# Attention with a written-out head loop: values of two tiles in one group, three score banks, and five tiles of each head summed by adding DMAs instead of TensorE

## What is computed

```python
scores = jnp.einsum('bhqd,bhkd->bhqk', q, k) * scale
probs = jax.nn.softmax(scores, axis=-1)
ctx = jnp.einsum('bhqk,bhkd->bhqd', probs, v)
```

## Time and profile before

| | |
|---|---|
| time, median of 3 runs | 2860.41 us (2859.59 to 2862.24) |
| profiled execution, its own time | 2861.7 us |
| span of its trace | 2859.9 us |
| PE busy (matmuls) | 2749.7 us, 96% |
| POOL busy | 1732.3 us, 61% |
| DVE busy | 1628.8 us, 57% |
| ACT busy | 1291.3 us, 45% |
| mean granted TensorE clock | 0.976 of full speed |

### The profile page before, as it was taken

One profiled execution on the slowest core, in us unless ns is written; L12 is line 12 of the kernel. 1 busy time (PEld: TensorE's weight loads), 2 busy tenths in 40 slices (PEclk: granted clock), 3 DMA queues, 4 the chain that ended last, 5 costly groups with the idle time before them and its releaser, 6 DMA issues. The chain is left out here.

```text
span 2859.9 us, 43470 instructions
## 1 busy us (share of the span) xinstructions
PE 2749.7 (96%) x13776; PEld 1609.4 (56%) x13776; DVE 1628.8 (57%) x2553; ACT 1291.3 (45%) x2299; POOL 1732.3 (61%) x406
## 2 busy tenths in 40 slices
PE   7999999999799999999999999999999999997999
PEld 6888887778344444444444444444444444436887
DVE  8411110111778777867777768767867777724231
ACT  3111111110066666656656656656656666672100
POOL 0111111110199989988989989889988998982111
PEclk9999999999599999999999999999999999998999
DMA  3233223112611121112111211221112111004332
GB/s 140 107 121 110 110 110 111 66 66 89 162 27 41 35 60 36 41 36 59 39 39 43 52 35 42 50 46 35 42 36 60 38 39 34 9 16 143 125 106 92
DMA packets 145917, 189.29 MB, mean 66 GB/s; under 512 B 87152, under 2 KB 112240, under 8 KB 134896
## 3 DMA queue, kind: packets, MB, share of 16 engines
q1 hardware_dynamic: 145712, 186.70, 23.5%
HBM read 122.44 MB, written 63.69 MB: 65 GB/s over the span
## 5 line engine op out<-in xcount | busy, mean ns | idle before, releaser
L859 DVE TENSOR_REDUCE part_max<-ps_b 128x1 f32<-128x512 f32 x2048 | 1275.9, 681 | 423.3 <-PE ps_b L740 420.3
L706 POOL TENSOR_TENSOR psum_p<-psum_p,probs 128x2048 f32<-128x2048 f32 x316 | 1457.7, 4613 | 30.4 <-ACT probs L837 0.5
L837 ACT ACTIVATE probs<-ps_b 128x512 f32<-128x512 f32 x2048 | 1115.6, 597 | 754.4 <-PE ps_b L730 724.3
L730 PE MATMUL ps_b<-qp,kp 97*128 97x512 f32 x2048 | 877.1, 432 | 1.5 <-ACT probs L837 1.5
L740 PE MATMUL ps_b<-kp,qp 96*128 96x512 f32 x2048 | 767.0, 417 | 62.6 <-DVE part_max L859 24.0
L730 PEld LDWEIGHTS ps_b<-qp,kp 97*128 97x128 f32 x2048 | 385.6, 189 | 622.1 <-ACT probs L837 460.3
L758 PE MATMUL ps_b<-probs,vh 128*32 128x512 f32 x4096 | 552.3, 611 | 2.6
L740 PEld LDWEIGHTS ps_b<-kp,qp 96*128 96x128 f32 x2048 | 399.1, 195 | 162.4 <-DVE part_max L859 68.1
L232 POOL TENSOR_TENSOR wlo<-wraw,whi 128x1024 fp32r<-128x1024 f32 x29 | 69.4, 2394 | 611.5 <-ACT whi L335 611.5
L261 PE MATMUL ps_a<-xhi,whi 128*128 128x512 f32 (+1 forms) x928 | 370.2, 399 | 1.0 <-DVE elo L424 0.9
L261 PE MATMUL ps_a<-xhi,wlo 128*128 128x512 f32 (+1 forms) x928 | 367.1, 396 | 0.0
(11 more groups left out here) (72 smaller groups left out, 1093.0 us busy)
## 6 DMA issues: line engine op xcount, KB each, us to landing
kp<-qk_scr SPq DMA_DIRECT2D x96, 256.0 KB, 4.1
qp<-qk_scr SPq DMA_DIRECT2D x96, 256.0 KB, 6.2
qk_scr<-ehi SPq DMA_DIRECT2D x16, 1024.0 KB, 3.9
qk_scr<-elo SPq DMA_DIRECT2D x16, 1024.0 KB, 6.7
wraw<-wcat SPq DMA_DIRECT2D x29, 512.5 KB, 7.5
craw<-cz_scr SPq DMA_DIRECT2D x16, 768.0 KB, 5.1
stage<-x SPq DMA_DIRECT2D x16, 512.0 KB, 4.5
v_scr<-elo SPq DMA_DIRECT2D x16, 512.0 KB, 3.3
```

Source lines behind the costliest of these rows:

```text
L706: pool.tensor_tensor(acc[:, :], (acc if n else probs[0])[:, :], probs[t % RING][:, :], ALU.add) \
L730: pe.matmul(ps[:, st_bank(g, j, b), :], kp[j][0:PACK + 1, t * P:(t + 1) * P], qp[j][0:PACK + 1, b * NQ:(b + 1) * NQ], start=True, stop=Tru ...
L837: act.activation(probs[t % RING][:, b * NQ:(b + 1) * NQ], ps[:, st_bank(g, j, b), :], ACT.Exp, scale=SCALE).then_inc(exp_done, 1)
L859: dve.tensor_reduce(part_max[jn % 2][:, tn, b:b + 1], ps[:, MAX_BANK + bank, :], AX_X, ALU.max) \
```

## The change

- All loops of `attend` are written out; there is no `Fori` left in it.
- Values of two tiles (t-2 and t-1) are computed in one group after every even step; transposed scores rotate over three banks (`n % 3`). The last head keeps one tile a step.
- Scores, the transposed maxima and the sums of a head share one ring of four banks in the order of use (`ring_order`); whoever comes to a bank waits for the reader of the unit four places before it (`wait_ring`).
- No tile is summed by TensorE except in the last head. POOL adds ten tiles into `psum_p` (nine additions). The exp of tile 0 is written to a tile of its own, `psum_q`, and five DMAs issued by POOL add tiles 2, 5, 8, 11, 14 onto it (`accum_op=ADD`, 128x2048 float32, 1 MB each), each waiting for the one before. TensorE multiplies `psum_q` and `psum_p` by ones after step 4 of the next head.
- `LEAD` (how many steps the maxima run ahead) is 4, was 3; three slots of q, k, v, were four. ACT takes the sums after step 5, the reciprocal comes after the maxima of step 9, and the product is cut into four instructions of 128x128, after the second maximum of steps 10, 11, 12 and 13.

```diff
-POOL_TILES = [0, 1, 2, 3, 4, 6, 7, 8, 9, 11, 12, 14]
+BASE_TILE = 0
+CHAIN_TILES = [2, 5, 8, 11, 14]
+POOL_TILES = [1, 3, 4, 6, 7, 9, 10, 12, 13, 15]
-LEAD = 3
-POOL_SUMS_AT, TAKE_SUMS_AT, RECIPROCAL_AT, NORMALISE_AT = 3, 4, 8, 10
+LEAD = 4
+SUMS_AT, TAKE_SUMS_AT, RECIPROCAL_AT, NORMALISE_AT = 4, 5, 9, 10
-        ST_BANKS, MAX_BANKS = 2, 4
-        MAX_BANK, PV_BANK, SUM_BANK = 2, 6, 7
+        ST_BANKS, RING_BANKS = 3, 4
+        RING_BANK, PV_BANK = 3, 7
+        def wait_ring(eng, u):
+            n = ring_place[u] - RING_BANKS
+            if n < 0:
+                return
+            kind, h = ring_order[n][:2]
+            if kind == "max":
+                eng.wait_ge(mx_free, maxima_until[n + 1])
+            elif kind == "sum":
+                eng.wait_ge(sums_taken, h + 1)
+            else:
+                eng.wait_ge(neg_ready, h + 1)
...
+            def chain(h, t):
+                if t == CHAIN_TILES[0]:
+                    pool.wait_ge(pv_done, TT * h + BASE_TILE + 1)
+                wait(pool, chained, chain_count(h, t) - 16)
+                pool.wait_ge(exp_done, 64 * h + 4 * t + 4)
+                pool.sem_inc(cleared, 1)
+                pool.dma_start(psum_q[h % 2][:, :], tile(h, t)[:, :], accum_op=ALU.add).then_inc(chained, 16)
+            for h in range(HEADS):
+                for t in range(TT):
+                    if h < LAST and t in CHAIN_TILES:
+                        chain(h, t)
+                    if t in pool_tiles(h)[1:]:
+                        add(h, t)
...
+            def sums(h):
+                u = ("sum", h, 0, 0)
+                wait_ring(pe, u)
+                pe.wait_ge(chained, chain_count(h, CHAIN_TILES[-1]))
+                sum_of(ring_bank(u), psum_q[h % 2], True, False)
+                pe.wait_ge(pool_done, pool_count(h, POOL_TILES[-1]))
+                sum_of(ring_bank(u), psum_p[h % 2], False, True).then_inc(sum_ready, 1)
+            def step(h, t):
+                for b in range(QB):
+                    if h >= 0:
+                        scores_t(h, t, b)
+                    if has_maxima(h, t):
+                        scores(h, t, b)
+                if h < 0:
+                    return
+                if t == 0 and h >= 1:
+                    values(h - 1, TT - 2)
+                    values(h - 1, TT - 1)
+                if h < LAST:
+                    if t % 2 == 0 and t >= 2:
+                        values(h, t - 2)
+                        values(h, t - 1)
...
+                if t == SUMS_AT and h >= 1:
+                    sums(h - 1)
...
+            for h in range(-1, HEADS):
+                for t in range(first_step(h), TT):
                     for b in range(QB):
+                        if has_maxima(h, t):
+                            take_max(h, t, b)
+                        if b == 1 and h >= 1 and 0 <= t - NORMALISE_AT < QB:
+                            normalise(h - 1, t - NORMALISE_AT)
+                    if t == RECIPROCAL_AT and h >= 1:
+                        reciprocal(h - 1)
```

More of the change, by code:

```diff
@@ L527, in attend @@
         psum_p = [sb(f"psum_p{s}", [P, T]) for s in range(2)]
+        psum_q = [sb(f"psum_q{s}", [P, T]) for s in range(2)]
         raw_ctx = [sb(f"raw_ctx{s}", [P, NQ]) for s in range(2)]
@@ L585, in target @@
[L585 to L618, removed]
+        def target(h, t):
+            return (h + 1, t + LEAD) if t + LEAD < TT else (h + 2, t + LEAD - TT)
@@ new lines, in has_maxima, with first_step @@
+        def has_maxima(h, t):
+            return target(h, t)[0] < HEADS
+        def first_step(h):
+            return 0 if h >= 0 else -LEAD
+        ring_order = []
+        for h in range(-1, HEADS):
+            for t in range(first_step(h), TT):
+                if has_maxima(h, t):
+                    ring_order += [("max", h, t, b) for b in range(QB)]
+                if t == SUMS_AT and h >= 1:
+                    ring_order.append(("sum", h - 1, 0, 0))
+                if t == TRANSPOSED_AT and h < LAST:
+                    ring_order.append(("flip", h + 1, 0, 0))
@@ L620, in attend, with tile @@
+        def tile(h, t):
+            return psum_q[h % 2] if based(h, t) else probs[slot(h, t)]
+        previous = {}
+        held = {}
+        for h in range(HEADS):
+            for t in range(TT):
+                if not based(h, t):
+                    previous[h, t] = held.get(slot(h, t))
+                    held[slot(h, t)] = (h, t)
         block = ctx.enter_context(nc.Block())
@@ L761, in values @@
+                if not (h == LAST and t in LAST_ONES_TILES):
                     last.then_inc(pv_done, 1)
-            def sums(g, j, t):
-                mine = tiles(g, j)[1]
-                if t not in mine:
-                    return
-                if t == mine[0]:
-                    wait(pe, sums_taken, number(g, j))
-                for b in range(QB):
-                    last = pe.matmul(ps[b * HD:(b + 1) * HD, SUM_BANK, :], ones[:, :],
-                                     probs[t % RING][:, b * NQ:(b + 1) * NQ], start=(t == mine[0]), stop=False)
-                last.then_inc(pv_done, 1)
@@ new lines, in _ @@
+            for h in range(-1, HEADS):
+                if h >= 0:
+                    pe.wait_ge(negmax_loaded[h % SLOTS], 16 * (h // SLOTS + 1))
+                for t in range(first_step(h), TT):
+                    step(h, t)
+                    if t == TRANSPOSED_AT and h < LAST:
+                        transpose_max(h + 1)
+            values(LAST, TT - 1)
+            last_sums(TT - 1)
+            pe.wait_ge(pool_done, pool_count(LAST, LAST_POOL_TILES[-1]))
+            sum_of(ring_bank(("sum", LAST, 0, 0)), psum_p[LAST % 2], False, True).then_inc(sum_ready, 1)
@@ L838, in period @@
                                        ACT.Exp, scale=SCALE).then_inc(exp_done, 1)
-                        if t == 0 and b == 3 and has_before:
-                            take_raw(*head(g, j, -1))
-                        if t == TAKE_SUMS_AT and b == 3 and has_before:
-                            take_sums(*head(g, j, -1))
-            for j in range(SLOTS):
-                period(0, j, j > 0)
-            with act.Fori(1, LAST[0]) as g:
-                for j in range(SLOTS):
-                    period(g, j)
@@ L872, in reciprocal @@
+            def reciprocal(h):
                 dve.wait_ge(sums_spread, 16 * QB * (h + 1))
@@ L918, in project_output @@
+                    if t == TRANSPOSED_AT and h < LAST:
+                        take_transposed(h + 1)
+            dve.wait_ge(sum_ready, HEADS)
+            dve.wait_ge(ctx_ready, QB * LAST)
+            dve.reciprocal(recip_b[:, :], ps[:, ring_bank(("sum", LAST, 0, 0)), :]).then_inc(recip_done, 1)
+            for part in range(QB):
+                normalise(LAST, part)
 def project_output(nc, x, w2, bias, cz_scr, w_early, early_loaded, out):
```

361 lines of the change are left out of this document (169 added, 192 removed).

## The result

The changed kernel takes 3005.9 us (median of four runs, 3000.9 to 3008.1) against 2860.1 us before: a ratio of 1.0507 [1.0494, 1.0519]. The forecast was 2940 us, so the sign was right, but the loss, +146 us, is nearly twice the +80 that I forecast. One execution of experiment 1, at 3028.2 us against 2967.0 for its fastest, counts as slow and is not in that experiment's ratio; all other executions that are compared are fast ones, but the single one of experiment 7, whose state is unknown.

A forecast was written before the change was run, and what follows sets the result against it. TensorE's order of issue was taken as the bound. A head: 49.1 + 1.5 + 5.7 + 2.5 + 0.3 = 59.1 us against 55.2; with 31 periods +121, jumps -39, leading maxima +2, odd heads -2: 2940 us, range 2800 to 3040.

The forecast's parts named there:

- The path without new waits: TensorE's issue through a head with paired values and two sum groups, nothing new waited for: 49.1 us a head.
- Sums in the ring: Step 5: a score takes the sums' bank and waits for ACT's late copy: +1.5 us a head.
- The jumps: Five jumps of the hardware loop, heads of 63.08 instead of 55.19 us, disappear when written out: -39 us.
- The sum: All terms together: 59.1 us a head against 55.2, whole kernel 2940 us.
- odd ones: Odd heads of the kernel before (a clock fall, last heads), set at -2 us in the total.
- The reciprocal's way: Steps 9 to 14: DVE waits 5.40 us from reciprocal to product, TensorE runs out of banks: +5.7 us a head.
- the adding DMAs: Five DMAs a head issued by POOL, expected to be hidden: +0.3 us a head, bounds 0 and 3.
- The price of a product: One DVE product of 128 columns in steps 10 to 13 costs 0.81 us, a quarter of 3.24.
- products blocked whole: Rival: each product on DVE waits for POOL's running addition, +6 us a head, about 3130 us; chance 0.04.
- Clock: New waits of TensorE make the granted clock fall to the lower level: +2.5 us a head, bounds 0 and 4.
- POOL: Rival: POOL becomes the bound from 3.4 us per adding DMA on; 3000 to about 3190 us; chance 0.08.

The follow-up runs named there:

- experiment 1: Changed kernel with the reciprocal two steps earlier (after step 7, was 9): 2967.0, 2967.5 and 2988.6 us, 1.0399 of the kernel before; 3028.2 us in the profiled execution.
- experiment 7: Changed kernel with the five DMAs of a head copying instead of adding (accum_op dropped): 2980.6 us in its one run.
- experiment 12: Experiment 5 with the seven loads issued in step 5, behind the spreading of the sums, and POOL's product after tile 12, not 9: 2708.0 us, 0.9465.
- experiment 4: Kernel before with its attention loops written out and nothing else: 2850.7 us, 0.9965.
- experiment 3: Changed kernel without the five adding DMAs of a head; POOL only counts up the semaphore: 2968.0 us, 1.0377 of the kernel before.
- experiment 5: Changed kernel with edits 1 and 2, the product as one POOL instruction after tile 9, and load_negmax issued ahead of the stores: 2768.4 us, 0.9669.
- experiment 9: Experiment 5 with the sums two steps later (steps 6, 7 and 9) and the product after tile 10: 2780.0 us, 0.9719.
- experiment 10: Changed kernel with only the product moved to POOL (one instruction after tile 9) and SP loading negated maxima before the stores: 2876.7 us, 1.0057.
- experiment 2: Experiment 1 with ACT's copy of the sums after the first exp of step 5, not the fourth: 2902.7 us, 1.0128.
- experiment 6: Experiment 2 with the product on DVE as one instruction of 512 columns in step 10, not four of 128: 2771.5 us, 0.9696.
- experiment 8: Kernel before, written out, with the product of a head on POOL behind its addition of tile 8: 2787.1 us, 0.9737.
- edits 1 and 2: In the changed kernel, reciprocal after step 7 instead of 9, and sums copied after the first exp of step 5: 2902.7 us with both.

## Why the prediction was right or wrong

**The path without new waits** (49.1 us a head) was right: bursts 5.79 us apart against 5.89, and the best heads of experiment 12 take 49.4. It would have been a gain of 6 us a head, and experiment 12 has 3.9 of it (51.3 against 55.2).

**Sums in the ring** (+1.5): right in place and mechanism, 1.3 measured in each of 30 heads.

**The jumps** (-39): the gaps are gone, as said, but writing them out by itself gave 10 (experiment 4). The sum took the period of the other heads for that of an unjumped kernel; but that period depends on where POOL's additions stand against the product, and this changed with the jumps (product 3.66 instead of 3.24 us). The sum had set the 55.6 us of the written-out heads of before aside as odd ones; they were the sign.

**The reciprocal's way** (+5.7, from 5.40 us) failed by way of the term beside it, *the adding DMAs* (+0.3, upper bound 3). I had written that they share the engines with the reciprocal's three steps, and put nearly nothing for it, without a row of any DMA of that kind. The runs showed 4.6 us more on that way (6.0 instead of 1.4 for the write), so that DVE waits 8.4 us, not 3.9, and TensorE 6.6, not 3.0. Here most products were cheap, since POOL stood idle by then. Together TensorE's waits for DVE are 7.3 us a head instead of 5.7. Experiments 1, 3 and 7 took the late landing away or shortened it.

**The price of a product** (0.81 us) rested on a misreading of rows 7, and so did the dismissal of the rival *products blocked whole*. I took 22 durations between 3.21 and 3.66 us as slowing, not as a wait. They were waits, and the trace of before shows it, POOL's addition beside the product of one head:

```profile
1720.60 4.57 POOL L706 TENSOR_TENSOR psum_p<-psum_p,probs 128x2048 f32<-128x2048 f32 x1
1722.48 3.25 DVE L889 TENSOR_TENSOR out_ctx<-raw_ctx,recip_b 128x512 f32<-128x512 f32 x1
```

The addition ends at 1725.17 and the product 0.56 us later, and so in all 31 products that start beside an addition: they end 0.55 to 0.56 us after it. POOL's additions stood at the same phase to the product in every head of the loop, so each block was the same. With another phase the same instruction takes 0.27 to 4.67 us, and, started beside an addition, it ends 0.15 to 0.16 us after it (all 29 such products of the changed kernel). The Trainium skill (SBUF — State Buffer, section Who interferes with whom) says that a DVE instruction with two SBUF inputs is blocked by a GpSimd instruction that reads SBUF until it ends; the traces agree with these numbers, and my argument against it did not hold. The rival's time (3130 us) wasn't reached, since POOL was idle at 99 of the 128 products.

**Clock** (+2.5): what remains of a head, 61.2 - 49.1 - 1.3 - 7.3 = 3.5 us, stands against 2.5 + 0.3. I had taken 2/3 and one fall of 3 us a head, about 5 us of low clock; in 30 heads the trace has 351.6 us of it, 11.7 a head, and TensorE works in 231.0 us of them, 7.7 a head. The 3.5 us are a remainder, but experiment 4 gives a price to hold against it: ten of its heads have one fall each, 34.1 us of low clock in all, and are about 1.5 us longer than the others. My estimate from this is 7.7 x 1.5 / 3.4 = 3.4 us a head.

**POOL** was rightly not the bound in the changed kernel (0.87 us for an issue against my 1 to 1.5). But the landing did matter: a DMA of 7.3 us (median) takes 11.5 beside the loads, and once the other waits were removed, the chain of five became the bound (experiments 5, 9 and 12). I had asked only whether the wait of one DMA hides behind POOL's additions, not whether the five and what they are issued between fit into the head.

**The sum**: 2.1 us a head too little, 7.3 instead of 5.7 for DVE and 3.5 instead of 2.8 for the clock and the rest, less 0.2 at the sums. Over 30 heads that is 63 us, which is the error (3006 - 2942 = 64). It closes because the clock's part is the remainder. The forecast's range held the time; of its terms, the path without waits and the sums in the ring were right, the reciprocal's way, the adding DMAs and the clock were too small, and that the wrong price of a product did little harm was luck: POOL happened to be idle at most of them.

**Open**: why a small write behind a 1 MB DMA lands only when that one does. That it lands 0.16 to 0.37 us after it at either distance (1.1 or 1.9 us), and after 1.4 us where it stands less than 0.5 us behind the issue (experiment 10), fits an order of the two and not a mere sharing of speed; no run was made to test it. The cost of the falls of the clock is an estimate.

## What to carry to other kernels

Durations that are equal in every repetition don't speak against a wait for another engine: in a locked rhythm a block is as constant as work. Lay the start and the end of the instruction beside those of the other engine in two places with different phases. Before a large DMA is added, look at every small one that is issued in the next microseconds and on which an engine waits; here its landing became the large one's. And an elementwise product of two SBUF tiles beside POOL's additions should be one instruction: going from four to one on DVE was worth 131 us (experiments 2 and 6). Moving it to POOL was worth 64 us in the kernel before, written out (experiments 4 and 8), and 3 us beside edits 1 and 2 (experiments 6 and 5); in experiment 10 the two and the new order on SP together gave 129.

## What the runs showed of the hardware

- A DVE product of two SBUF tiles (128x128) takes 0.28 us with POOL idle and up to 4.67 us beside POOL's addition of 128x2048, and then ends 0.15 us after it; one of 128x512 ends 0.55 us after it.
- An adding DMA of 1 MB from SBUF to SBUF lands after 7.3 us, a copy after 4.7 (medians), and with 1.75 MB of loads around it the adding one takes 11.5. The adding one occupied POOL for 0.87 us, the copy for 0.57.
- An 8 KB write, 1.4 us alone, landed after 3.1 us behind the copy and after 6.0 behind the adding DMA (0.16 to 0.37 us after that one), and after 10.4 behind seven loads in its own queue.
- In a wait of TensorE of 6.6 us the granted clock fell to 0.50, and it was back at 1.00 only 5.6 us after TensorE had started again.
- Ten heads with one fall of the clock each took 1.5 us more than heads without (experiment 4).
